# Attention denominators: summing four steps instead of two before the matmul with ones

## The chip, the cores and the metric

The kernel runs on one core of one Trainium2 chip. The metric is the device time of one execution in microseconds (us). Three runs of the kernel before gave 4889.07, 4887.17 and 4884.74 us, so the median is 4887.17 us.

A core has five engines that follow their own instruction lists and meet only at semaphores: TensorE (PE, matrix multiply, writes PSUM), VectorE (DVE), ScalarE (ACT), GpSimd (POOL) and the SyncE queue (SP) that issues transfers. PEld is the loading of weights into TensorE.

## The reference, cut to what matters

The whole kernel is a chain of four layers on x of shape 16 x 128 x 32 x 32. The change lies in one block, the attention of the third layer, on 16 batches of 1024 tokens:

```python
sq = (x @ wq_s).reshape(b, n, S, DH).transpose(0, 2, 1, 3) * scale     # S = 8 heads, DH = 16
sk = (x @ wk_s).reshape(b, n, S, DH).transpose(0, 2, 1, 3)
rv = (x @ wv_r).reshape(b, n, R, DH).transpose(0, 2, 1, 3)             # R = 2 retrievals
search_sim = jnp.einsum('bsid,bsjd->bsij', sq, sk)
search_attn = jax.nn.softmax(search_sim, axis=-1)
retrieved = jnp.einsum('bsij,brjd->bsird', search_attn, rv)
...
out = jnp.einsum('bsir,bsird->bsid', retrieval_attn, retrieved)
return out.transpose(0, 2, 1, 3).reshape(b, n, S * DH) @ w_out
```

The softmax over j (1024 keys) needs a sum of exponentials for each query i: the denominator. It is this sum that the change computes in another order.

## The kernel before, in words

`phase_attn` works through 16 batches. A batch has 32 steps `k`. A step takes one block of 128 keys for four heads and 512 queries, and eight steps in a row cover all 1024 keys of those heads and queries, so four groups of eight steps make a batch. All loops over batches are unrolled by two.

In step `k` TensorE does, in this order (function `slot` of the tensor block):

- four times a score matmul of step `k + 2` (`score`, into one of three PSUM tiles `at_S`), and between them the side work of step `k`. Scores run two steps ahead.
- the side work (`fill`): in almost every step four tiles of scores of the next batch, from which the row maxima are taken ("max"), and in a few steps transposes that finish an earlier half batch ("tokens", "back"), the output matmul ("wout") and the row offsets ("rows"). Side tiles go round three PSUM banks `at_side`.
- in every second step, in the middle of the step, `totals`: four matmuls with a matrix of ones that add 128 keys of a pair sum into `at_den`.
- `values`: four matmuls of the exponentials with the values, into `at_num`.

ScalarE (`exps`) turns the scores of a step into exponentials, tile by tile, into one of four slots `at_P`. A score matmul waits until the exponential three tiles back has been taken. At an even step `exps` also waits (`pair_done`) until the pair that used those slots four steps earlier has been added.

GpSimd (`pair`) adds the slots of two steps, 128 x 2048 elements, into `at_pairs` 0 or 1: pair `i` belongs to steps `2i` and `2i + 1`. Between pairs it does one part of seven of the small retrieval attention (`retrieve`). VectorE (`drain`) takes the maximum of each "max" tile and empties the other side tiles in the order in which TensorE made them. So VectorE is always at the step of TensorE or just behind it, while ScalarE and GpSimd work on later steps.

Names and lines of the profile: `at_S` L1633 score, `at_side` L1600 "max" tile, `at_den` L1655 totals, `at_num` L1644 values, `at_P` L1772 exponential, `at_pairs` L1532 pair sum, `at_mx` L1699 maximum, L1545 to L1570 the parts of `retrieve`.

Of the kernel before, what the change touches and what calls it, by code (L numbers as in the profile page):

```python
# [13 lines left out]
ALU = mybir.AluOpType  # L14
# [4 lines left out]
B = 16  # L19
# [1292 lines left out]
SIDES = 3  # L1312
RING = 3
HEADS = STEPS * 4
TOKENS_AT = (3, 19)
BACK_AT = (5, 22)
WOUT_AT = (6, 23)
EXP_AT = (28, 12)
SUM_AT = (30, 14)
MAX_AT = 19  # L1320
ROWS_AT = (27, 3, 11, 19)
GROUP = 32
# [44 lines left out]
def phase_attn(nc, K, D, X):  # L1367
# [6 lines left out]
    with Mem(nc, "at") as m:  # L1374
# [29 lines left out]
        side_ready, side_saved = m.sem("side_ready"), m.sem("side_saved")  # L1404
        s_ready, p_ready, pv_done = m.sem("s_ready"), m.sem("p_ready"), m.sem("pv_done")
        pair_done, den_done = m.sem("pair_done"), m.sem("den_done")
        num_saved, den_saved = m.sem("num_saved"), m.sem("den_saved")
        row_step, row_ready = m.sem("row_step"), m.sem("row_ready")
        far_ready = m.sem("far_ready")
# [46 lines left out]
        with nc.Block() as block:  # L1456
# [65 lines left out]
            @block.gpsimd  # L1522
            def _(g):
                for u in range(2):
                    g.memset(ko[u][KQ:KM, :, :], 1.0).then_inc(const_ready, 1)

                def pair(b, i):

                    wait_if(g, den_done, 16 * b + i - 1)
                    g.wait_ge(p_ready, HEADS * b + 8 * i + 8)  # L1530
                    a = 2 * i % SLOTS
                    g.tensor_tensor(pairs[i % 2][:, :, :], P[a][:, :, :], P[a + 1][:, :, :], ALU.add).then_inc(pair_done, 1)  # L1532

                def retrieve(b, h, part, tokens):

                    done = (0, 1, 4, 7, 7, 9, 10)[part]
                    step = Chain(g, post_step, 11 * (2 * b + h) + done)
                    heads = prod[:, :, :].rearrange("p i (s d) -> p (i s) d", d=DH)
                    nv = numT[:, :, :].rearrange("p i (s r d) -> p (i s) r d", r=RH, d=DH)
                    pv = prod[:, :, :].rearrange("p i (s r d) -> p (i s) r d", r=RH, d=DH)  # L1540
                    rec = recT
                    if part == 0:
                        g.wait_ge(side_saved, tokens)
                        g.wait_ge(u_in[h], 16 * b + 16)
                        step(g.tensor_tensor(pv, nv, ub[h][:, :, :].rearrange("p i (s o d) -> p (i s) o d", o=1, d=DH)  # L1545
                                             .to_broadcast([C, 32, RH, DH]), ALU.mult))
                    elif part == 1:
                        for w in (8, 4, 2):
                            step(g.tensor_tensor(heads[:, :, 0:w], heads[:, :, 0:w], heads[:, :, w:2 * w], ALU.add))
                    elif part == 2:  # L1550
                        step(g.tensor_tensor(sim[:, :, :].rearrange("p s r -> p (s r)"), heads[:, :, 0], heads[:, :, 1], ALU.add))
                        step(g.tensor_tensor(sim[:, :, :], sim[:, :, :],
                                             rec[:, :].rearrange("p (s o) -> p s o", o=1).to_broadcast([C, 32, 2]), ALU.mult))

                        step(g.tensor_tensor(sm1[:, :], sim[:, :, 0], sim[:, :, 1], ALU.subtract))
                        g.sem_inc(sim_ready, 1)
                    elif part == 3:
                        g.wait_ge(e_ready, 2 * b + h + 1)
                        g.tensor_tensor(sm1[:, :], sim[:, :, 0], sim[:, :, 1], ALU.add).then_inc(esum_ready, 1)
                    elif part == 4:  # L1560
                        g.wait_ge(rsum_ready, 2 * b + h + 1)
                        step(g.tensor_tensor(sm1[:, :], sm1[:, :], rec[:, :], ALU.mult))
                        step(g.tensor_tensor(sim[:, :, :], sim[:, :, :],
                                             sm1[:, :].rearrange("p (s o) -> p s o", o=1).to_broadcast([C, 32, 2]), ALU.mult))
                    elif part == 5:
                        step(g.tensor_tensor(heads, numT[:, :, :].rearrange("p i (s d) -> p (i s) d", d=DH),
                                             sim[:, :, :].rearrange("p s (r o) -> p (s r) o", o=1).to_broadcast([C, 64, DH]),
                                             ALU.mult))
                    else:
                        step(g.tensor_tensor(ub[h][:, :, :].rearrange("p i (s d) -> p (i s) d", d=DH),  # L1570
                                             pv[:, :, 0, :], pv[:, :, 1, :], ALU.add))
                        g.sem_inc(out_ready, 1)

                def slot(b, u, last):
                    post = not is_first(b)
                    for i in range(16):
                        pair(b, i)
                        if i == 0 and post:
                            retrieve(b - 1, 0, 6, None)
                        if 2 <= i <= 8 and post:  # L1580
                            retrieve(b - 1, 1, i - 2, side_at(b, ("tokens", 1, 3), last))
                        if i >= 10:
                            retrieve(b, 0, i - 10, side_at(b, ("tokens", 0, 3), last))

                over(g, B, slot)
                retrieve(B - 1, 0, 6, None)
                for part in range(7):
                    retrieve(B - 1, 1, part, TAIL_BASE + 4)

            @block.tensor  # L1590
            def _(pe):
# [55 lines left out]

                def totals(b, k):

                    j = (k - 2) % 8  # L1650
                    if j == 0:
                        wait_if(pe, den_saved, 4 * b + k // 8)
                    pe.wait_ge(pair_done, 16 * b + k // 2)
                    for i in range(QUAD):
                        last = pe.matmul(den[32 * i:32 * i + 32, :], K["ones"][:, 0:32], pairs[(k // 2 - 1) % 2][:, i, :],  # L1655
                                         start=(j == 0), stop=(j == 6))
                    last.then_inc(den_done, 1)

                for n in range(LEAD):
# [6 lines left out]
                def slot(b, u, last):  # L1666
# [5 lines left out]
                    for k in range(STEPS):  # L1672
                        if not last and k in (MAX_AT, MAX_AT + 8):
                            pe.wait_ge(op_in[1 - u][(k - MAX_AT) // 8], loads(b + 1, 1 - u))
                        work = side_work(k, first, last)
                        ahead_of = (b, u, k + 2) if k + 2 < STEPS else None if last else (b + 1, 1 - u, k + 2 - STEPS)
                        for i in range(QUAD):
                            if ahead_of:
                                score(*ahead_of, i)
                            for w in work[(i * len(work) + 2) // 4:((i + 1) * len(work) + 2) // 4]:  # L1680
                                fill(w, b, u, side_free(b, at), at % SIDES).then_inc(side_ready, 1)
                                at += 1
                            if i == 1 and k % 2 == 0 and not (first and k == 0):
                                totals(b, k)
                        values(b, u, k)

                over(pe, B, slot)
                totals(B, 0)
                for at, w in enumerate(TAIL):
                    fill(w, B, 0, side_free(B, at), at % SIDES).then_inc(side_ready, 1)  # L1690

# [1 line left out]
            def _(v):  # L1693
                def drain(w, b, u, at, bank):
# [36 lines left out]
                    else:  # L1731
                        xb = X[:, bass.ds((b - 1) * N + w[1] * CH, CH)]
                        v.tensor_tensor(xb, xb, side[bank][:, :], ALU.add).then_inc(side_saved, 1)

                def invert(job):
                    v.wait_ge(esum_ready, job + 1)
                    v.reciprocal(sm1[:, :], sm1[:, :]).then_inc(rsum_ready, 1)
# [5 lines left out]
                def slot(b, u, last):  # L1743
                    first = is_first(b)
                    at = 0
                    for k in range(STEPS):
                        if k == SUM_AT[1] and not first:
                            invert(2 * b - 1)
                        if k == SUM_AT[0]:
                            invert(2 * b)  # L1750
                        for w in side_work(k, first, last):
                            drain(w, b, u, side_base(b) + at, at % SIDES)
                            at += 1

                over(v, B, slot)
                for at, w in enumerate(TAIL):
                    if w == ("back", 1):
                        invert(2 * B - 1)
                    drain(w, B, 0, TAIL_BASE + at, at % SIDES)

            @block.scalar
            def _(a):
# [11 lines left out]
                def save(b, g, what):  # L1774
# [6 lines left out]
                            a.wait_ge(side_ready, side_at(b, ("tokens", 1 - half, 3), isinstance(b, int) and b == B - 1))  # L1781
                        a.copy(sums[:, quad, :], num[:, :]).then_inc(num_saved, 1)
                    else:
                        a.wait_ge(den_done, 16 * b + 4 * g + 4)
                        a.copy(sums[:, 2 + quad, :], den[:, :]).then_inc(den_saved, 1)

                def softmax2(job):
# [7 lines left out]
                def slot(b, u, last):  # L1795
# [2 lines left out]
                        exps(b, 0)  # L1798
                    for k in range(STEPS):
                        saved = None  # L1800
                        if k % 8 < 2 and (k >= 8 or not first):
                            saved = (b, k // 8 - 1, k % 8) if k >= 8 else (b - 1, 3, k % 8)
                        if k + 1 < STEPS:
                            exps(b, k + 1, saved)
                        elif not last:
# [1012 lines left out]
```

## Time and profile before

| | |
|---|---|
| median of three runs | 4887.17 us |
| the profiled execution | 4881.74 us |
| its span, first to last instruction | 4879.9 us |
| busy PE, DVE, ACT, POOL over the span | 86%, 60%, 45%, 37% |
| mean granted TensorE clock | 0.921 |

The page gives busy shares over the whole program, which runs through several phases; what the attention block does is read from its own stretch. The attention steps lie between 1258 and 3216 us of the span. A granted clock of 1.0 is 2.4 GHz, one of 0.5 is 1.2 GHz. Busy time of PE counts a pipelined matmul up to its end, so two matmuls in a row overlap, and the distance between their starts is what one costs.

### The profile page before, as it was taken

To read this page: it belongs to the slowest core of one execution; us is meant where nothing else is said; L and a number is where in the kernel's file an instruction comes from. 1 tells how busy PE (TensorE), PEld (TensorE's weight loads), DVE (VectorE), ACT (ScalarE), POOL (GpSimd) and SP (SyncE) were. 2 spreads that over 40 slices of the span, in tenths; PEclk is the share of its full clock that TensorE was granted. 3 is DMA by queue.
4 is the path that set the end of the run, shared out by engine and by line. 5 is a ranking of instruction groups with operands and counts; after the bars stand their busy time and mean duration, and the time that the engine had idled before them with its cause. 6 is when DMAs were issued, how large, how long until landed. Compare 5 with 4: busy or idle time off the path is not lost. (4 is left out here: it accounts for less than half of the span.)

```text
span 4879.9 us, 76343 instructions
## 1 busy us (share of the span) xinstructions
PE 4184.0 (86%) x23099; PEld 1656.3 (34%) x23099; DVE 2925.3 (60%) x5621; ACT 2181.0 (45%) x4040; POOL 1827.4 (37%) x1333
## 2 busy tenths in 40 slices
PE   5799999846999999999999999967999999876513
PEld 2343433324222222222222222234444444453312
DVE  4788888656777777777777777742000000256774
ACT  3333333245466656565656566653333333431400
POOL 1100000037477777777777777771000000220401
PEclk9999999979899999999999999988999999966655
DMA  3555645357322222222222222010000000111504
GB/s 138 138 137 118 140 115 136 74 195 253 42 33 33 33 33 33 33 33 33 33 33 33 33 33 33 6 61 29 0 0 0 0 0 0 74 65 47 190 0 151
DMA packets 201952, 313.47 MB, mean 64 GB/s; under 512 B 48887, under 2 KB 132861, under 8 KB 199181
## 3 DMA queue, kind: packets, MB, share of 16 engines
q1 hardware_dynamic: 172296, 270.23, 23.8%
q10 hardware_dynamic: 24960, 28.87, 1.7%
q0 software_dynamic: 4368, 10.07, 0.7%
q8 instruction: 197, 3.23, 0.3%
q14 instruction: 131, 1.07, 0.1%
HBM read 102.88 MB, written 78.12 MB: 37 GB/s over the span
## 5 line engine op out<-in xcount | busy, mean ns | idle before, releaser
L1699 DVE TENSOR_REDUCE at_mx<-at_side 128x1 f32<-128x512 f32 x2048 | 1295.6, 682 | 410.0 <-PE at_side L1600 402.5
L1772 ACT ACTIVATE at_P<-at_S 128x512 f32<-128x512 f32 x2048 | 1115.2, 600 | 702.3 <-PE at_S L1633 692.6
L1532 POOL TENSOR_TENSOR at_pairs<-at_P 128x2048 f32<-128x2048 f32 x256 | 1159.9, 4531 | 238.5 <-ACT at_P L1772 210.7
L1633 PE MATMUL at_S<-at_qo,at_ko 99*128 99x512 bf16 x2048 | 788.2, 387 | 73.3 <-ACT at_P L1772 47.6
L1600 PE MATMUL at_side<-at_ko,at_qo 96*128 96x512 bf16 x2048 | 775.8, 389 | 29.3 <-DMA at_ko<-qk 24.1
L2054 ACT ACTIVATE ff_hs<-ff_ph,ff_b 128x512 f32<-128x512 f32 x512 | 351.7, 687 | 524.4 <-PE ff_ph L2024 524.4
L1644 PE MATMUL at_num<-at_P,at_rvt 128*32 128x512 f32 x4096 | 557.5, 606 | 0.0
L2024 PE MATMUL ff_ph<-ffn_Y,ff_w 128*128 (+1 forms) x1024 | 524.8, 594 | 8.7 <-DMA ff_b<-in_b_dram 8.7
L2038 PE MATMUL ff_po<-ff_hs,ff_w2s 128*128 128x512 f32 x1024 | 522.5, 592 | 0.0
L2073 DVE SCALAR_TENSOR_TENSOR X<-ff_po,ffn_b2w,X 128x512 f32 (+1 forms) x32 | 24.0, 751 | 822.9 <-PE ff_po L2038 822.9
L834 DVE SCALAR_TENSOR_TENSOR la_dwq<-la_pad,la_taps,la_dwq 128x1024 f32<-128x1024 f32 x384 | 491.4, 1280 | 11.1
L1633 PEld LDWEIGHTS at_S<-at_qo,at_ko 99*128 99x128 bf16 x2048 | 198.2, 97 | 879.3 <-ACT at_P L1772 658.0
L1108 POOL TENSOR_TENSOR n_ln_ab<-n_ln_mv,eps 128x4 f32<-128x4 f32 x96 | 19.1, 199 | 1161.0 <-DVE n_ln_mv L1099 1158.3
L582 POOL DMA_DIRECT2D proj<-la_y x32 | 17.4, 544 | 810.3 <-ACT la_y L941 810.3
L619 PE MATMUL la_acc<-la_rep,la_wagg 128*32 128x512 f32 x2560 | 314.6, 609 | 3.8 <-DMA la_rep<-la_pad 3.1
L1600 PEld LDWEIGHTS at_side<-at_ko,at_qo 96*128 96x128 bf16 x2048 | 200.9, 98 | 272.0 <-DVE at_mx L1699 95.0
L2024 PEld LDWEIGHTS ff_ph<-ffn_Y,ff_w 128*128 128x128 f32 x1024 | 195.3, 191 | 254.4 <-issue 245.0
L1655 PE MATMUL at_den<-at_pairs,ones 128*32 128x512 f32 x2048 | 277.3, 614 | 4.5 <-POOL at_pairs L1532 4.4
L2038 PEld LDWEIGHTS ff_po<-ff_hs,ff_w2s 128*128 128x128 f32 x1024 | 194.6, 190 | 245.2 <-issue 244.7
L1123 ACT ACTIVATE n_ln_xt<-n_ln_front,n_ln_ab 128x128 f32<-128x128 f32 x384 | 144.4, 456 | 114.2 <-POOL n_ln_ab L1114 103.8
L1644 PEld LDWEIGHTS at_num<-at_P,at_rvt 128*32 128x32 f32 x4096 | 91.3, 108 | 174.7 <-issue 104.3
L1545 POOL TENSOR_TENSOR at_prod<-at_numT,at_ub 128x1024 f32<-128x1024 f32 x32 | 75.5, 2358 | 185.0 <-DVE at_recT L1728 185.0
(416 smaller groups left out, 4596.4 us busy)
## 6 DMA issues: line engine op xcount, KB each, us to landing
la_rep<-la_pad SPq DMA_DIRECT2D x512, 162.8 KB, 3.6
qk<-ap_part SPq DMA_DIRECT2D x32, 768.0 KB, 3.7
at_qo<-qk SPq DMA_DIRECT2D x384, 64.0 KB, 3.7
at_ko<-qk SPq DMA_DIRECT2D x192, 128.0 KB, 5.8
n_ln_xs<-X SPq DMA_DIRECT2D x96, 256.0 KB, 2.3
u<-ap_us SPq DMA_DIRECT2D x32, 320.0 KB, 4.0
X<-in_x_dram SPq DMA_DIRECT2D x4, 2048.0 KB, 25.6
conv<-conv_Y SPq DMA_DIRECT2D x16, 512.0 KB, 2.6
```

Source lines behind the costliest of these rows:

```text
L619: done = pe.matmul(acc[c][32 * j:32 * j + 32, :], wagg[:, p - 1, j, g, :], view(slice(0, C), p, h, j, *PLACES[g]), start=(c < 2 and g == 0 ...
L834: v.scalar_tensor_tensor(out, image, taps[:, t:t + 1], out, ALU.mult, ALU.add).then_inc(tap_done, 1)
L1532: g.tensor_tensor(pairs[i % 2][:, :, :], P[a][:, :, :], P[a + 1][:, :, :], ALU.add).then_inc(pair_done, 1)
L1600: return pe.matmul(side[bank][:, :], qo[of_u][0:KQ, i // QUAD, s, i % QUAD * C:(i % QUAD + 1) * C], ko[of_u][0:KQ, s, h * CH:(h + 1) * CH] ...
L1633: pe.matmul(S[n % RING][:, :], ko[u][:, h, j * C:(j + 1) * C], qo[u][:, half, h, :], start=True, stop=True).then_inc(s_ready, 1)
L1644: last = pe.matmul(num[32 * i:32 * i + 32, :], rvt[u][:, j, :], P[k % SLOTS][:, i, :], start=(j == 0), stop=(j == 7))
L1655: last = pe.matmul(den[32 * i:32 * i + 32, :], K["ones"][:, 0:32], pairs[(k // 2 - 1) % 2][:, i, :], start=(j == 0), stop=(j == 6))
L1699: v.reduce_max(mx[:, n // 2, n % 2:n % 2 + 1], side[bank][:, :], AX.X).then_inc(side_saved, 1)
L1772: a.activation(P[k % SLOTS][:, i, :], S[(4 * k + i) % RING][:, :], ACT.Exp).then_inc(p_ready, 1)
L2024: pe.matmul(ph[j % R][:, :], w1[:, f, :], Y[:, bass.ds(b * N + half * CH, CH)], start=True, stop=True).then_inc(h_mm, 1)
L2038: done = pe.matmul(po[half][:, :], w2s[u][:, f, :], hs[j % R][:, :], start=(f == 0), stop=(f == FT - 1)).then_inc(h_used, 1)
L2054: a.activation(hs[j % R][:, :], ph[j % R][:, :], ACT.Gelu, bias=b1[:, j % FT:j % FT + 1]).then_inc(h_ready, 1)
```

## The change

The pair sums are added once more before the matmul with ones: the sum of an even pair (`at_pairs0`) is added onto the sum of the odd pair after it (`at_pairs1`), so that `totals` runs once for four steps. The second addition has 128 x 2048 elements too. GpSimd does its left half (two of four heads, 128 x 1024) right behind the odd pair; VectorE does the right half as two instructions of 128 x 512 (`right`), one at the end of steps 4, 8, 12, ..., one behind the second side tile of steps 5, 9, 13, ... The next even pair waits for both halves, the next odd pair for `totals`. Positions of other work are moved by the table of constants and in the lists of GpSimd and ScalarE.

```diff
-TOKENS_AT = (3, 19)
-BACK_AT = (5, 22)
-WOUT_AT = (6, 23)
-EXP_AT = (28, 12)
-SUM_AT = (30, 14)
+TOKENS_AT = (4, 20)
+BACK_AT = (9, 25)
+WOUT_AT = (10, 26)
+EXP_AT = (30, 14)
+SUM_AT = (31, 16)
...
                 def pair(b, i):
 
-                    wait_if(g, den_done, 16 * b + i - 1)
+                    if i % 2 == 0:
+                        wait_if(g, quad_right, 16 * b + i)
+                        wait_if(g, quad_left, 8 * b + i // 2)
+                    else:
+                        wait_if(g, den_done, 8 * b + i // 2)
                     g.wait_ge(p_ready, HEADS * b + 8 * i + 8)
                     a = 2 * i % SLOTS
                     g.tensor_tensor(pairs[i % 2][:, :, :], P[a][:, :, :], P[a + 1][:, :, :], ALU.add).then_inc(pair_done, 1)
+                    if i % 2:
+                        g.wait_ge(pair_done, 16 * b + i + 1)
+                        g.tensor_tensor(pairs[1][:, 0:2, :], pairs[1][:, 0:2, :], pairs[0][:, 0:2, :], ALU.add).then_inc(quad_left, 1)
...
-                        if i == 0 and post:
-                            retrieve(b - 1, 0, 6, None)
-                        if 2 <= i <= 8 and post:
-                            retrieve(b - 1, 1, i - 2, side_at(b, ("tokens", 1, 3), last))
-                        if i >= 10:
-                            retrieve(b, 0, i - 10, side_at(b, ("tokens", 0, 3), last))
+                        if i < 2 and post:
+                            retrieve(b - 1, 0, 5 + i, None)
+                        if 3 <= i <= 9 and post:
+                            retrieve(b - 1, 1, i - 3, side_at(b, ("tokens", 1, 3), last))
+                        if i >= 11:
+                            retrieve(b, 0, i - 11, side_at(b, ("tokens", 0, 3), last))
...
                 def totals(b, k):
 
-                    j = (k - 2) % 8
-                    if j == 0:
-                        wait_if(pe, den_saved, 4 * b + k // 8)
-                    pe.wait_ge(pair_done, 16 * b + k // 2)
+                    q = (k - 6) // 4
+                    if q % 2 == 0:
+                        wait_if(pe, den_saved, 4 * b + q // 2)
+                    pe.wait_ge(quad_left, 8 * b + q + 1)
+                    pe.wait_ge(quad_right, 16 * b + 2 * q + 2)
...
-                            if i == 1 and k % 2 == 0 and not (first and k == 0):
+                            if i == 1 and k % 4 == 2 and not (first and k == 2):
                                 totals(b, k)
...
+                def right(b, q, i):
+
+                    v.wait_ge(pair_done, 16 * b + 2 * q + 2)
+                    v.tensor_tensor(pairs[1][:, i, :], pairs[1][:, i, :], pairs[0][:, i, :], ALU.add).then_inc(quad_right, 1)
...
-                        for w in side_work(k, first, last):
+                        work = side_work(k, first, last)
+                        for i, w in enumerate(work):
                             drain(w, b, u, side_base(b) + at, at % SIDES)
                             at += 1
+                            if i == min(1, len(work) - 1) and k % 4 == 1 and not (first and k == 1):
+                                right(b, (k - 5) // 4, 3)
+                        if not work and k % 4 == 1:
+                            right(b, (k - 5) // 4, 3)
+                        if k % 4 == 0 and not (first and k == 0):
+                            right(b, (k - 4) // 4, 2)
...
-                        if k % 8 < 2 and (k >= 8 or not first):
-                            saved = (b, k // 8 - 1, k % 8) if k >= 8 else (b - 1, 3, k % 8)
+                        if k % 8 in (0, 3) and (k >= 8 or not first):
+                            what = int(k % 8 == 3)
+                            saved = (b, k // 8 - 1, what) if k >= 8 else (b - 1, 3, what)
```

On GpSimd, at the start of a batch, the list of the kernel before goes through the pairs (L1532) with a part of the retrieval between them:

```order
L1532 TENSOR_TENSOR at_pairs1<-at_P2,at_P3 128x2048
L1566 TENSOR_TENSOR at_prod<-at_numT,at_sim 128x1024
L1532 TENSOR_TENSOR at_pairs0<-at_P0,at_P1 128x2048
L1570 TENSOR_TENSOR at_ub1<-at_prod 128x512
...
L1545 TENSOR_TENSOR at_prod<-at_numT,at_ub0 128x1024
```

The same place of GpSimd's list in the changed kernel, from one even pair to the next (L1537 is the pair, L1540 the left half of the second addition):

```order
L1537 TENSOR_TENSOR at_pairs0<-at_P0,at_P1 128x2048
L1537 TENSOR_TENSOR at_pairs1<-at_P2,at_P3 128x2048
L1540 TENSOR_TENSOR at_pairs1<-at_pairs1,at_pairs0 128x1024
L1553 TENSOR_TENSOR at_prod<-at_numT,at_ub0 128x1024
...
L1557 TENSOR_TENSOR at_prod<-at_prod 128x64x8
```

An instruction of 128 x 1024 now stands behind every odd pair, and the even pair that follows writes the tile `at_pairs0` that VectorE's halves read.

On VectorE, in steps 8 and 9 of a batch, the changed kernel has the two instructions of `right` (L1748) between the maxima (L1709) of the side tiles; before, the eight maxima followed each other. Each row names the bank of the side tile that it empties:

```order
L1709 TENSOR_REDUCE at_mx<-at_side2 128x1
L1709 TENSOR_REDUCE at_mx<-at_side0 128x1
L1709 TENSOR_REDUCE at_mx<-at_side1 128x1
L1748 TENSOR_TENSOR at_pairs1<-at_pairs1,at_pairs0 128x512
L1709 TENSOR_REDUCE at_mx<-at_side2 128x1
L1709 TENSOR_REDUCE at_mx<-at_side0 128x1
L1748 TENSOR_TENSOR at_pairs1<-at_pairs1,at_pairs0 128x512
L1709 TENSOR_REDUCE at_mx<-at_side1 128x1
```

The first `right` stands behind the last maximum of step 8, the second behind the second maximum of step 9.

## Rows read from the trace of the kernel before

**Rows 1.** The page's groups: out<-in count | busy, mean ns | idle before, releaser

```profile
L1699 DVE TENSOR_REDUCE at_mx<-at_side 128x1 f32<-128x512 f32 x2048 | 1295.6, 682 | 410.0 <-PE at_side L1600 402.5
L1772 ACT ACTIVATE at_P<-at_S 128x512 f32<-128x512 f32 x2048 | 1115.2, 600 | 702.3 <-PE at_S L1633 692.6
L1532 POOL TENSOR_TENSOR at_pairs<-at_P 128x2048 f32<-128x2048 f32 x256 | 1159.9, 4531 | 238.5 <-ACT at_P L1772 210.7
L1655 PE MATMUL at_den<-at_pairs,ones 128*32 128x512 f32 x2048 | 277.3, 614 | 4.5 <-POOL at_pairs L1532 4.4
```

**Rows 2.** Tile at_S: ns min/median/max of an instruction, first and last start

```profile
L1633 PE MATMUL at_S<-at_qo,at_ko x2048: 377/381/634, 1258.3 to 3214.9; 99*128 99x512 bf16 x187
```

**Rows 3.** Waits, 1258 to 3230 us: who for whom, us in total, times, longest

```profile
PE at_S L1633 <- ACT at_P L1772: 47.6, 66, 1.4
...
ACT at_P L1772 <- POOL at_pairs L1532: 1.5, 2, 1.1
```

**Rows 4.** Windows, one batch: us; busy PE, PEld, DVE, ACT, POOL; clock, DMA

```profile
1625.00:1748.00 123.00, 114.40 (x676) 33.56 (x668) 90.44 (x167) 72.29 (x138) 91.41 (x41) 0.99 0.23 34
```

**Rows 5.** Timeline of two plain steps: start, duration, engine, instruction, idle before

```profile
1753.79 0.39 PE L1633 MATMUL at_S<-at_qo,at_ko 99*128 99x512 bf16 x1
...
1754.44 2.48 DVE L1699 TENSOR_REDUCE at_mx<-at_side 128x1 f32<-128x512 f32 x4 [0.69 <-PE at_side L1600]
...
1755.11 0.38 PE L1633 MATMUL at_S<-at_qo,at_ko 99*128 99x512 bf16 x1
...
1756.64 0.39 PE L1633 MATMUL at_S<-at_qo,at_ko 99*128 99x512 bf16 x1
...
1757.61 1.06 PE L1655 MATMUL at_den<-at_pairs,ones 128*32 128x512 f32 x8
...
1758.61 0.39 PE L1633 MATMUL at_S<-at_qo,at_ko 99*128 99x512 bf16 x1
```

**Rows 6.** Timeline around the latest pair of a batch, steps 21 to 24

```profile
1701.67 2.40 ACT L1772 ACTIVATE at_P<-at_S 128x512 f32<-128x512 f32 x4 [0.89 <-PE at_S L1633]
...
1709.37 4.53 POOL L1532 TENSOR_TENSOR at_pairs<-at_P 128x2048 f32<-128x2048 f32 x1 [0.23 <-POOL at_prod L1545]
...
1713.49 0.39 PE L1633 MATMUL at_S<-at_qo,at_ko 99*128 99x512 bf16 x1
...
1714.18 2.07 ACT L1772 ACTIVATE at_P<-at_S 128x512 f32<-128x512 f32 x4
...
1714.84 0.39 PE L1633 MATMUL at_S<-at_qo,at_ko 99*128 99x512 bf16 x1 [0.74 <-ACT at_P L1772]
```

**Rows 7.** Groups of GpSimd by shape: the costliest part of retrieve

```profile
L1545 POOL TENSOR_TENSOR at_prod<-at_numT,at_ub 128x1024 f32<-128x1024 f32 x32 | 75.5, 2358 | 185.0 <-DVE at_recT L1728 185.0
```

**Rows 8.** Groups of VectorE by shape: additions with both inputs in SBUF

```profile
L2539 DVE TENSOR_TENSOR sk_tmp<-sk_G,sk_vv 128x1024 f32<-128x1024 f32 x8 | 9.8, 1225 | 0.3
...
L761 DVE TENSOR_TENSOR X<-X,la_res 128x512 f32<-128x512 f32 x8 | 5.1, 684 | 0.0
```

**Rows 9.** Timeline of PE: matmuls that start after an idle time

```profile
750.50 5.82 PE L598 MATMUL la_acc<-X,la_wqkv 128*128 x9 [2.05 <-issue]
...
1748.13 0.60 PE L1633 MATMUL at_S<-at_qo,at_ko 99*128 99x512 bf16 x1 [4.47 <-issue]
```

**Rows 10.** Windows, columns as in Rows 4, behind and around those idle times

```profile
751.71:755.12 3.41, 3.41 (x5) 1.35 (x4) 3.30 (x4) 1.35 (x3) 0.00 (x0) 0.51 0.97 208
1745.00:1750.00 5.00, 1.86 (x8) 0.56 (x12) 0.69 (x1) 1.27 (x3) 4.62 (x2) 0.50 1.11 134
```

**Rows 11.** Timeline: a VectorE copy within SBUF beside a GpSimd memset

```profile
4587.63 1.80 POOL L2413 MEMSET sk_zeros<- 128x2048 f32 x1 [0.15 <-POOL sk_gw L2411]
4587.80 1.71 DVE L2509 COPY sk_same_e<-sk_emask 128x128 f32<-128x128 f32 x1
```

**Rows 12.** Timeline: VectorE products with both inputs in SBUF beside GpSimd

```profile
138.09 6.43 POOL L571 TENSOR_SCALAR_AFFINE_SELECT la_plain<-la_plain 32x128 f32<-32x128 f32 x8
...
140.28 3.02 DVE L784 TENSOR_TENSOR la_wagg<-la_pwt,la_dwt 128x1280 f32<-128x1280 f32 x2
```

More of the change, by code:

```diff
@@ L1406, in phase_attn @@
         pair_done, den_done = m.sem("pair_done"), m.sem("den_done")
+        quad_left, quad_right = m.sem("quad_left"), m.sem("quad_right")
         num_saved, den_saved = m.sem("num_saved"), m.sem("den_saved")
@@ L1577, in slot @@
                         pair(b, i)
-                        if i == 0 and post:
-                            retrieve(b - 1, 0, 6, None)
-                        if 2 <= i <= 8 and post:
-                            retrieve(b - 1, 1, i - 2, side_at(b, ("tokens", 1, 3), last))
-                        if i >= 10:
-                            retrieve(b, 0, i - 10, side_at(b, ("tokens", 0, 3), last))
+                        if i < 2 and post:
[4 more added lines that the diff above has]
+                            retrieve(b, 0, i - 11, side_at(b, ("tokens", 0, 3), last))
                 over(g, B, slot)
-                retrieve(B - 1, 0, 6, None)
+                for part in range(5, 7):
+                    retrieve(B - 1, 0, part, None)
                 for part in range(7):
@@ L1648, in totals @@
                 def totals(b, k):
-                    j = (k - 2) % 8
-                    if j == 0:
-                        wait_if(pe, den_saved, 4 * b + k // 8)
-                    pe.wait_ge(pair_done, 16 * b + k // 2)
+                    q = (k - 6) // 4
[3 more added lines that the diff above has]
+                    pe.wait_ge(quad_right, 16 * b + 2 * q + 2)
                     for i in range(QUAD):
-                        last = pe.matmul(den[32 * i:32 * i + 32, :], K["ones"][:, 0:32], pairs[(k // 2 - 1) % 2][:, i, :],
-                                         start=(j == 0), stop=(j == 6))
+                        last = pe.matmul(den[32 * i:32 * i + 32, :], K["ones"][:, 0:32], pairs[1][:, i, :],
+                                         start=(q % 2 == 0), stop=(q % 2 == 1))
                     last.then_inc(den_done, 1)
@@ L1687, in _ @@
                 over(pe, B, slot)
-                totals(B, 0)
+                totals(B, 2)
                 for at, w in enumerate(TAIL):
@@ L1750, in slot @@
                             invert(2 * b)
-                        for w in side_work(k, first, last):
+                        work = side_work(k, first, last)
+                        for i, w in enumerate(work):
                             drain(w, b, u, side_base(b) + at, at % SIDES)
                             at += 1
+                            if i == min(1, len(work) - 1) and k % 4 == 1 and not (first and k == 1):
[4 more added lines that the diff above has]
+                            right(b, (k - 4) // 4, 2)
                 over(v, B, slot)
+                for i in range(2, 4):
+                    right(B, -1, i)
                 for at, w in enumerate(TAIL):
@@ L1783, in save @@
                     else:
-                        a.wait_ge(den_done, 16 * b + 4 * g + 4)
+                        a.wait_ge(den_done, 8 * b + 2 * g + 2)
                         a.copy(sums[:, 2 + quad, :], den[:, :]).then_inc(den_saved, 1)
```

## The prediction

> **What bounds the kernel now.** First the page's groups, for the size of each instruction of the attention block [rows 1], then the tile `at_S`, for how long the block lasts. Its first score starts at 1258.3 us and its last at 3214.9 [rows 2]: 1956.6 us for 16 batches of 32 steps, which is 15.29 us for four steps (a quad; there are 128). All terms below are per quad.
>
> The windows of one batch show no idle engine to spare except ScalarE: of 123 us PE is busy 114, DVE 90, POOL 91 and ACT 72 [rows 4]. The timeline of plain steps gives TensorE's price. A step without totals runs from 1753.79 to 1756.64, 2.85 us; a totals group occupies it from 1757.61 to 1758.61, 1.00 us [rows 5]. A quad with two totals is 4 x 2.85 + 2 x 1.00 = 13.4 us. The other 1.9 us of the 15.29 are the tokens, back, wout and rows work, the restart of the loop every second batch and short waits. So TensorE's own list bounds the block. The waits agree: the scores wait 47.6 us in all for exponentials, and ScalarE waits 1.5 us in all for a pair [rows 3].
>
> That GpSimd holds nobody up rests on slack, and the slack can be read. Pair 11 (steps 22 and 23) is the latest of its batch. The exponentials of step 23 end at 1701.67 + 2.40 = 1704.07, in TensorE's step 21, but the pair starts only at 1709.37, since GpSimd had waited for tokens, and ends at 1713.90. Step 24 of TensorE begins at 1713.49, and the exponentials that reuse the slots begin at 1714.18 [rows 6]. So a pair may start as late as the end of the step behind the one in which its last operand was scored (here step 22), and no later: these 5.3 us were just early enough.
>
> **The change part by part.**
>
> *TensorE loses work.* The 2048 rows of L1655 [rows 1] are 256 totals groups of 8; half go, one per quad: 1.00 us less. Its list falls from 13.4 to 12.4 us.
>
> *GpSimd gains the left half*, 128 x 1024. With 2.36 us for 1024 columns [rows 7] and 4.53 for 2048 [rows 1], I take 2.3 us (an estimate; L1545 reads in a more broken pattern, so it is at the upper end). Its load per batch goes from 91.4 to 91.4 + 8 x 2.3 = 110 us, 13.7 per quad: more than TensorE's plain list, less than 15.29. By load alone it fits.
>
> *VectorE gains two additions of 128 x 512* at 0.68 us each [rows 8]. Load per batch: 90.4 + 16 x 0.68 = 101 us, 12.7 per quad. Fits too.
>
> *The new wait is what counts.* The even pair of a quad (steps 0 and 1 of the quad) now waits until VectorE has added both halves of the quad before. The second of these stands behind the second side tile of step 1, and VectorE gets a side tile only when TensorE has computed it in step 1. But the exponentials of step 1 are done two steps earlier, while TensorE is in step 3 of the quad before. So an even pair can no longer start early. It starts when TensorE is at the end of step 1, and its 4.53 us then lie across step 2, in which TensorE scores the next quad's step 0, whose exponentials need the slots of this very pair. By rows 6 the latest harmless start was the end of step 0. Queued behind the waiting pair are the retrieval part, the odd pair and the next left half; ScalarE waits for the pair, TensorE for ScalarE.
>
> This closes a loop whose length is the period of a quad:
> - even pair 4.53 [rows 1];
> - first exponential of the next step 0: 0.60 [rows 1];
> - from the fourth score of step 2, which waits for that exponential (three score tiles go ahead), to the end of step 2: 1756.64 - 1755.11 = 1.53 [rows 5];
> - step 3: 2.85;
> - from the start of the next step 0 to its first maximum: 1754.44 - 1753.79 = 0.65 [rows 5];
> - four maxima 2.48 [rows 5], first addition 0.68, two maxima of step 1 1.24 (half of 2.48), second addition 0.68.
>
> The sum is 15.24. Three changes of engine (VectorE to GpSimd, to ScalarE, to TensorE) at about 0.1 each make 15.5; one is read as 1714.84 - 1714.18 - 0.60 = 0.06 [rows 6]. TensorE's list of 12.4 us lies beside it, so TensorE stands still for 3.1 us in every step 2. The totals that were saved fall into that hole and buy nothing.
>
> *Extras.* Of the 1.9 us beyond the plain list, some falls on the loop (tokens in steps 0 and 3, the rows work on VectorE in step 3 which delays step 0's maxima, the copy of `at_num` in step 0, long retrieval parts before the odd pair) and some into the hole (tokens and wout in step 2). Bounds 0 and 1.9; I take half, 0.95, since two of the four steps lie on the loop whole and two in part.
>
> *The clock.* TensorE now idles 3.1 us at a stretch. Before two matmuls of the trace it had idled 2.05 and 4.47 us [rows 9], and the granted clock was 0.51 in the 3.41 us behind the first and 0.50 around the second [rows 10]: 1.2 in place of 2.4 GHz. Such a stretch costs half of 3.41 us, 1.7, where TensorE works through it, and nothing where it stands still anyway. Bounds 0 and 1.7; I take 0.9, in the middle, because the slow stretch begins partly inside the hole, and steps 2 and 3 behind it lie on the loop.
>
> *Moved positions.* Tokens one step later, back and wout three or four, each part of the retrieval one pair later, the two copies into `at_sums` apart: as many instructions as before. They cost nothing while GpSimd waits for VectorE anyway; were that cover gone, the longest part, 2.36 us [rows 7], would delay an odd pair, which is counted among the extras. At the end one left half and two additions follow the last pair, some 4 us once.
>
> Sum: 15.5 + 0.95 + 0.9 = 17.35 against 15.29, 2.06 more; times 128 is 264 us. The profiled execution took 4881.7 us (span 4879.9), so 5146; the median of the runs is 5.4 above it. With that, 5150.
>
> **The rivals.**
>
> 1. *Only the loop.* Extras all in the hole, no clock loss: 15.5, 0.2 us x 128 = 27 us more, about 4915; with a part of the extras up to 5000. For it: the clock stood at 0.99 over a batch that is full of short waits [rows 4]. Against it: the rows work lies in step 3 of every second quad, and 2.05 us of idling were enough to lose the clock [rows 9, 10].
>
> 2. *VectorE's additions are held by GpSimd.* A copy within SBUF of 128 x 128 took 1.71 us and ended at 4589.51, with a GpSimd memset that ended at 4589.43 [rows 11]; it seems to have waited it out. Against: two products with two SBUF inputs, 128 x 1280, took 3.02 us, 1.51 each, beside GpSimd selects without a gap [rows 12], just what 684 and 1225 ns for 512 and 1024 columns [rows 8] extrapolate to (1.50). If held, the first addition waits for the left half or a retrieval part under way, from 0 to 2.3 us; the second does not, as GpSimd then waits for it. Since GpSimd's work behind the odd pair ends near the time of the first addition, I take 0.6: 77 us more than forecast, 5225; at the upper end 5440.
> The Trainium skill, "SBUF — State Buffer", section "SBUF: two separate sides", says that a VectorE instruction with two SBUF inputs and a GpSimd instruction that reads SBUF exclude each other for a whole instruction. By that rule it is this rival. Rows 11 agree with an exclusion, rows 12 do not.
>
> 3. *Faster.* If the new wait ended before the pair could start anyway, TensorE's list would still bind: 15.29 - 1.00 = 14.3, 128 us less, 4754. For it: every engine's load fits into 14.3 (GpSimd 13.7). It decides by whether the second addition ends before the end of step 0; its place in VectorE's list, behind two side tiles of step 1, speaks against.
>
> **How the numbers follow.** Forecast (loop, extras, some clock; 5000 to 5310) 0.68; rival 1 0.11; rival 2 0.10; rival 3 0.11. Range 4940 to 5310: the lower end leaves out rival 3 and the bottom of rival 1, the upper end takes in the middle of rival 2. The largest sum of the upper bounds, 15.5 + 1.9 + 1.7 + 2.3 = 21.4, would be 5670 and is left out. About 10 us (0.2%) is what runs of this kernel can tell from no change. Faster: rival 3, 0.11. Same: the very bottom of rival 1, 0.03. Slower 0.86.
>
> **What would show it.** In the profile after: GpSimd's pair waits for VectorE's `at_pairs` some 100 times, hundreds of us in all; ScalarE's wait for `at_pairs` grows from 1.5 us to several hundred (about 4 us x 128); the scores' wait for `at_P` on TensorE grows by about 3 us x 128; the clock in a batch falls from 0.99 to about 0.9 or less; L1655 has 1024 rows. Extras and clock can be told apart by the length of step 3. An addition of VectorE that lasts much over 0.7 us speaks for rival 2. ScalarE without a wait for `at_pairs` would prove me wrong.

## The result, and the profile after

The changed kernel took 5242.77 us (median of four runs, 5232.06 to 5251.3), the kernel before on the same chip 4885.95 us (four runs, 4883.24 to 4889.07). The ratio is 1.0729 [1.0704, 1.0754]: slower by 357 us, where 264 were forecast. The profiled execution has a span of 5234.2 us and a mean granted clock of 0.888, against 4879.9 and 0.921.

The tile `at_S` of the changed kernel gives the length of the block (ns min/median/max, first and last start):

```profile
L1642 PE MATMUL at_S<-at_qo,at_ko x2048: 379/389/634, 1258.0 to 3560.0; 99*128 99x512 bf16 x187
```

That is 2302.0 us in place of 1956.6 [rows 2], 17.98 us per quad in place of 15.29: 345 of the 354 us by which the span grew lie here.

The page's groups that answer to [rows 1] (out<-in count | busy, mean ns | idle before, releaser), with the two halves of the second addition:

```profile
L1709 DVE TENSOR_REDUCE at_mx<-at_side 128x1 f32<-128x512 f32 x2048 | 1308.2, 682 | 608.6 <-PE at_side L1609 604.6
L1796 ACT ACTIVATE at_P<-at_S 128x512 f32<-128x512 f32 x2048 | 1107.9, 605 | 1057.9 <-POOL at_pairs L1537 661.5
L1537 POOL TENSOR_TENSOR at_pairs<-at_P 128x2048 f32<-128x2048 f32 x256 | 1155.3, 4518 | 570.5 <-ACT at_P L1796 323.7
...
L1540 POOL TENSOR_TENSOR at_pairs<-at_pairs 128x1024 f32<-128x1024 f32 x128 | 302.3, 2362 | 10.0
...
L1748 DVE TENSOR_TENSOR at_pairs<-at_pairs 128x512 f32<-128x512 f32 x256 | 190.4, 744 | 13.6 <-POOL at_pairs L1537 13.6
```

No engine fills the new length: over the block PE is busy 1941 of 2302 us, GpSimd 1743, VectorE 1605 (first window below). What grew is idle time; the three old groups shown here all have more of it, and their instructions are about as long as before. The additions of VectorE, 744 ns in the mean, are longer than the 684 ns of [rows 8].

The waits of the changed kernel over the block (who for whom, us in total, times, longest), against [rows 3]:

```profile
ACT at_P L1796 <- POOL at_pairs L1537: 661.5, 158, 5.0
...
PE at_S L1642 <- ACT at_P L1796: 330.4, 218, 3.0
POOL at_pairs L1537 <- ACT at_P L1796: 323.7, 86, 46.2
...
POOL at_pairs L1537 <- DVE at_pairs L1748: 240.6, 58, 15.3
```

ScalarE waited 1.5 us for pairs before and waits 661.5 now. The pair's own wait is split over two names. A wait for several semaphores is put down to the one that came last by the profile, which here is often ScalarE's exponential; but that exponential belongs to a later step than the pair. In the 124 quads where the timeline shows all of it, the even pair starts 0.22 us (mean) behind the end of VectorE's second addition.

One turn of the loop in the timeline (start, duration, engine, instruction, idle before), from step 0 into the next step 3:

```profile
1694.02 0.68 DVE L1748 TENSOR_TENSOR at_pairs<-at_pairs 128x512 f32<-128x512 f32 x1
...
1694.73 1.29 DVE L1709 TENSOR_REDUCE at_mx<-at_side 128x1 f32<-128x512 f32 x2
...
1695.94 0.68 DVE L1748 TENSOR_TENSOR at_pairs<-at_pairs 128x512 f32<-128x512 f32 x1
...
1696.87 4.51 POOL L1537 TENSOR_TENSOR at_pairs<-at_P 128x2048 f32<-128x2048 f32 x1 [4.02 <-DVE at_pairs L1748]
...
1701.49 1.08 ACT L1796 ACTIVATE at_P<-at_S 128x512 f32<-128x512 f32 x2 [4.91 <-POOL at_pairs L1537]
...
1702.15 0.61 PE L1642 MATMUL at_S<-at_qo,at_ko 99*128 99x512 bf16 x1 [2.63 <-ACT at_P L1796]
...
1703.11 1.94 PE L1653 MATMUL at_num<-at_P,at_rvt 128*32 128x512 f32 x8
...
1720.39 0.39 PE L1642 MATMUL at_S<-at_qo,at_ko 99*128 99x512 bf16 x1 [1.73 <-ACT at_P L1796]
...
1720.93 1.06 PE L1653 MATMUL at_num<-at_P,at_rvt 128*32 128x512 f32 x8
```

Addition, two maxima, addition, pair, exponential, score: each row starts within 0.3 us of the end of the one before it (for the score, of the first of the two exponentials), and GpSimd, ScalarE and TensorE had stood idle 4.02, 4.91 and 2.63 us until then. Behind the idle time of 2.63 us the eight value matmuls took 1.94 us, one quad later, behind 1.73 us, 1.06. The granted clock was 0.50 around the first, which is 1.2 GHz, and 1.00 around the second.

Windows of the changed kernel: the whole block, those two places, and two stretches of 135 us (columns as in [rows 4]):

```profile
1258.00:3560.00 2302.00, 1941.28 (x9925) 550.12 (x9925) 1605.47 (x2903) 1173.68 (x2262) 1742.78 (x746) 0.91 0.17 25
1703.00:1705.00 2.00, 2.00 (x10) 0.23 (x10) 0.88 (x2) 1.05 (x3) 1.84 (x2) 0.50 1.14 125
1720.90:1722.10 1.20, 1.20 (x10) 0.31 (x10) 0.69 (x1) 0.91 (x2) 1.20 (x1) 1.00 0.00 0
...
1651.00:1786.00 135.00, 113.73 (x626) 33.56 (x626) 100.43 (x186) 73.36 (x142) 108.87 (x49) 0.97 0.21 30
2056.00:2191.00 135.00, 113.54 (x563) 33.57 (x560) 91.02 (x166) 65.11 (x125) 100.34 (x43) 0.87 0.20 30
```

The clock is not lost evenly: 0.97 in one stretch, 0.87 in another, 0.91 over the block, where it was 0.99 before.

### The profile page after: what moved, and what is told of

Same layout as the page of the kernel before. It is cut to its first block and busy times, and to the rows that moved or that the text cites. A ratio compares the mean times of both kernels' runs of the same rounds, so it can differ in the third digit from the quotient of the medians.

```text
span 5234.2 us, 74930 instructions
## 1 busy us (share of the span) xinstructions
PE 4247.1 (81%) x22075; PEld 1662.8 (32%) x22075; DVE 3090.6 (59%) x5877; ACT 2166.2 (41%) x4040; POOL 2136.8 (41%) x1461
## 5 line engine op out<-in xcount | busy, mean ns | idle before, releaser
L1709 DVE TENSOR_REDUCE at_mx<-at_side 128x1 f32<-128x512 f32 x2048 | 1308.2, 682 | 608.6 <-PE at_side L1609 604.6
L1796 ACT ACTIVATE at_P<-at_S 128x512 f32<-128x512 f32 x2048 | 1107.9, 605 | 1057.9 <-POOL at_pairs L1537 661.5
L1537 POOL TENSOR_TENSOR at_pairs<-at_P 128x2048 f32<-128x2048 f32 x256 | 1155.3, 4518 | 570.5 <-ACT at_P L1796 323.7
L1642 PE MATMUL at_S<-at_qo,at_ko 99*128 99x512 bf16 x2048 | 848.1, 416 | 362.3 <-ACT at_P L1796 330.4
L1609 PE MATMUL at_side<-at_ko,at_qo 96*128 96x512 bf16 x2048 | 811.6, 416 | 28.7 <-DMA at_ko<-qk 24.3
L1653 PE MATMUL at_num<-at_P,at_rvt 128*32 128x512 f32 x4096 | 625.8, 674 | 0.0
L834 DVE SCALAR_TENSOR_TENSOR la_dwq<-la_pad,la_taps,la_dwq 128x1024 f32<-128x1024 f32 x384 | 491.3, 1279 | 11.1
L1540 POOL TENSOR_TENSOR at_pairs<-at_pairs 128x1024 f32<-128x1024 f32 x128 | 302.3, 2362 | 10.0
L1748 DVE TENSOR_TENSOR at_pairs<-at_pairs 128x512 f32<-128x512 f32 x256 | 190.4, 744 | 13.6 <-POOL at_pairs L1537 13.6
```

The source lines that it names most:

```text
L834: v.scalar_tensor_tensor(out, image, taps[:, t:t + 1], out, ALU.mult, ALU.add).then_inc(tap_done, 1)
L1540: g.tensor_tensor(pairs[1][:, 0:2, :], pairs[1][:, 0:2, :], pairs[0][:, 0:2, :], ALU.add).then_inc(quad_left, 1)
L1609: return pe.matmul(side[bank][:, :], qo[of_u][0:KQ, i // QUAD, s, i % QUAD * C:(i % QUAD + 1) * C], ko[of_u][0:KQ, s, h * CH:(h + 1) * CH] ...
L1642: pe.matmul(S[n % RING][:, :], ko[u][:, h, j * C:(j + 1) * C], qo[u][:, half, h, :], start=True, stop=True).then_inc(s_ready, 1)
L1653: last = pe.matmul(num[32 * i:32 * i + 32, :], rvt[u][:, j, :], P[k % SLOTS][:, i, :], start=(j == 0), stop=(j == 7))
L1709: v.reduce_max(mx[:, n // 2, n % 2:n % 2 + 1], side[bank][:, :], AX.X).then_inc(side_saved, 1)
```

## The experiments

The theory was the loop: even pair, exponential, rest of step 2, step 3, the maxima and additions up to the second addition, and round again, with a clock loss in the hole of step 2. The main rival was that VectorE's additions and GpSimd's instructions hold each other up; another was that the moved positions cost something. All times below are medians; ratios are to the kernel before on the same chip (4886.71 us, seven runs, for the first four; 4887.97, seven runs, for the last two).

**Both additions one position earlier.** They stand at the end of step 0, so the loop loses the two maxima of step 1:

```diff
-                            if i == min(1, len(work) - 1) and k % 4 == 1 and not (first and k == 1):
-                                right(b, (k - 5) // 4, 3)
...
                         if k % 4 == 0 and not (first and k == 0):
-                            right(b, (k - 4) // 4, 2)
+                            for i in range(2, 4):
+                                right(b, (k - 4) // 4, i)
```

> Both additions of VectorE stand at the end of step 0 of a quad; the second no longer waits behind two maxima of step 1. Loop theory: the two maxima (1.24 us) leave the loop and TensorE's hole in step 2 gets as much shorter, with some clock back: 1.2 to 1.8 us per quad, 128 quads, so 5010 to 5090 us. Rival (the added load on GpSimd and VectorE and their exclusion is the cost, not the place of the wait): within 15 us of 5243.

One run: 4980.48 us, clock 0.918; 262 us less than the changed kernel, and below the loop's expectation. Its waits over the block:

```profile
ACT at_P L1793 <- POOL at_pairs L1537: 487.9, 158, 4.9
...
POOL at_pairs L1537 <- DVE at_pairs L1748: 181.1, 81, 11.4
...
PE at_S L1642 <- ACT at_P L1793: 145.6, 159, 3.3
```

The loop is still closed, only shorter. The block's scores start from 1257.0 to 3303.4 us: 15.99 per quad, 1.99 less. The two maxima are 1.24 of it. Over the block the clock is 0.98 in place of 0.91, so most of the other 0.75 is likely the clock; that is argued, not measured apart. Against the kernel with the hole filled (below), whose clock is as high, the move is worth 17.03 - 15.99 = 1.04 us.

**Additions before the even pair needs them.** Both at the end of step 3 of their own quad, which should open the loop altogether:

```diff
...
+                        if k % 4 == 3:
+                            for i in range(2, 4):
+                                right(b, (k - 3) // 4, i)
...
```

> Both additions of VectorE stand at the end of step 3 of their own quad, a whole step and a half earlier. Loop theory: the even pair can start about when its operands are ready, the loop no longer sets the period, and TensorE's list with half the totals (14.3 us) or GpSimd and VectorE taking turns (about 15.1 us if they exclude each other) does: 4760 to 4870 us, ScalarE's wait for pairs under 100 us, clock near 0.98. Rival (added load and exclusion cost the time): above 5000 us.

5305.5 us, ratio 1.0854 [1.0818, 1.089]: slower than the changed kernel, and the loop's expectation failed. The waits of this kernel:

```profile
POOL at_pairs L1537 <- PE at_den L1665: 415.7, 117, 6.6
...
PE at_side L1609 <- DVE at_mx L1709: 208.2, 89, 3.1
...
ACT at_P L1791 <- POOL at_pairs L1537: 11.1, 4, 4.8
```

The additions of this kernel (tile `at_pairs`, ns min/median/max):

```profile
L1748 DVE TENSOR_TENSOR at_pairs<-at_pairs x256: 676/1379/2851, 1273.2 to 3648.1; 128x512 f32<-128x512 f32 x128
```

And its timeline at one pair of additions:

```profile
2029.21 2.35 POOL L1540 TENSOR_TENSOR at_pairs<-at_pairs 128x1024 f32<-128x1024 f32 x1
...
2030.02 2.09 DVE L1748 TENSOR_TENSOR at_pairs<-at_pairs 128x512 f32<-128x512 f32 x1
...
2031.52 2.79 POOL L1553 TENSOR_TENSOR at_prod<-at_numT,at_ub 128x1024 f32<-128x1024 f32 x1
...
2032.03 2.83 DVE L1748 TENSOR_TENSOR at_pairs<-at_pairs 128x512 f32<-128x512 f32 x1
...
2035.52 0.61 PE L1609 MATMUL at_side<-at_ko,at_qo 96*128 96x512 bf16 x1 [3.11 <-DVE at_mx L1709]
```

Two additions of 0.68 us take 4.84. The first ends 0.55 us behind the left half's end (2031.56); then the retrieval part, 2.36 us elsewhere, takes 2.79, and the second ends 0.55 behind that (2034.86). The maxima behind them in VectorE's list come late, TensorE finds no free side bank for 3.11 us, and the totals, which stand in step 2 of a TensorE that is now late, hold the odd pair: 117 of the 128 odd pairs wait for them. These additions in turn wait for the odd pair, so this is a loop again, over the other wait that the change brought in. ScalarE's wait for pairs is down to 11.1 us, as the loop theory wanted; the bound that takes its place is dearer. Part of the time is the clock, 0.86 over the block against 0.91 in the changed kernel; how much was not taken apart.

**The hole filled.** The changed kernel with two more groups of totals per quad, on weights of zero, in step 2 (2.0 us of TensorE work more per quad, the sums unchanged):

```diff
...
+                    for _ in range(2):
+                        last = group(nothing[:, :], False, False)
...
```

> The changed kernel with two more groups of totals matmuls on zero weights behind the real one, in step 2 of each quad: 2.0 us more work for TensorE per quad, 256 us in all, put where it stands still. Loop theory with a clock cost: the hole absorbs the work, the granted clock stays up (0.90 to about 0.97 in the block) and the time falls by 0.5 to 1.5 us per quad, to 5050 to 5180 us. Loop theory without a clock cost: 5243, within 15 us. Rival (TensorE's work still sets the period): 256 us more, 5500 us.

5115.77 us, ratio 1.0467 [1.045, 1.0485], clock 0.922: 127 us less than the changed kernel although it does 256 us of matmuls more. The waits for the loop stay (GpSimd's pair is L1540 in this kernel, the exponential L1807):

```profile
ACT at_P L1807 <- POOL at_pairs L1540: 669.9, 163, 5.0
```

The window of the whole block, in this kernel:

```profile
1260.00:3440.00 2180.00, 2000.85 (x11941) 590.50 (x11941) 1598.13 (x2903) 1163.20 (x2261) 1749.03 (x746) 0.99 0.18 27
```

The clock is 0.99, as in the kernel before (1.00 and 0.95 in the two stretches of 135 us). The loop alone thus costs 17.03 us per quad (scores from 1260.4 to 3440.2 us), and the clock that the changed kernel loses 0.95 on top.

**Positions only.** The kernel before with the changed table of constants and the moved parts of the retrieval, without the second addition:

```diff
-TOKENS_AT = (3, 19)
+TOKENS_AT = (4, 20)
...
-                        if 2 <= i <= 8 and post:
+                        if 3 <= i <= 9 and post:
```

> The kernel before with only the moved positions of the change (tokens, back, wout, exponentials and reciprocals of the retrieval, and its parts one pair later); sums of two steps and all totals as before. Forecast: positions cost nothing, 4886 us within 15. Rival: they are part of the loss, above 4920 us.

One run: 4880.12 us, clock 0.921; the runs of before lie between 4880.9 and 4890.76. These moves cost nothing in the kernel before. The moved copies of ScalarE into `at_sums` are not among them, and in the changed kernel no run takes the moves apart.

**Additions in the middle of step 0,** both behind its second side tile:

```diff
-                            if i == min(1, len(work) - 1) and k % 4 == 1 and not (first and k == 1):
-                                right(b, (k - 5) // 4, 3)
+                            if i == min(1, len(work) - 1) and k % 4 == 0 and not (first and k == 0):
+                                for half in range(2, 4):
+                                    right(b, (k - 4) // 4, half)
...
```

> Both additions of VectorE behind the second side tile of step 0. Loop theory alone: two more maxima (1.24 us) leave the loop compared with the end of step 0 (period 15.99 us there), which brings it to about 14.7, near TensorE's own list: 4790 to 4850 us. If VectorE's addition and a GpSimd instruction that reads SBUF exclude each other: the additions now come while the left half (2.36 us) runs on GpSimd, last over 1 us on average in place of 0.74, VectorE falls behind and TensorE waits for side tiles: 4880 to 5050 us.

5014.3 us, ratio 1.0259 [1.0242, 1.0276], clock 0.909. By the loop alone it should have beaten the end of step 0, and it is 34 us slower than that one run; it lies where exclusion was to bring it. Its waits, and its additions:

```profile
ACT at_P L1796 <- POOL at_pairs L1537: 213.6, 106, 4.9
...
POOL at_pairs L1537 <- DVE at_pairs L1748: 116.8, 78, 8.3
POOL at_pairs L1537 <- PE at_den L1665: 108.5, 54, 5.1
```

```profile
L1748 DVE TENSOR_TENSOR at_pairs<-at_pairs x256: 677/781/2864, 1279.1 to 3345.6; 128x512 f32<-128x512 f32 x128
```

ScalarE's wait for pairs falls to a third of the changed kernel's, and odd pairs wait for totals. The additions last 1.12 us in the mean, as expected under exclusion. The loop is still there: 107 of 127 even pairs start within 0.4 us behind the second addition. The clock over the block is 0.96, against 0.98 with the additions at the end of step 0, so that part of the 34 us is the clock too.

**All of the second addition on VectorE,** two instructions of 128 x 1024 in the same place, nothing of it on GpSimd:

```diff
-                        g.tensor_tensor(pairs[1][:, 0:2, :], pairs[1][:, 0:2, :], pairs[0][:, 0:2, :], ALU.add).then_inc(quad_left, 1)
...
-                    v.tensor_tensor(pairs[1][:, i, :], pairs[1][:, i, :], pairs[0][:, i, :], ALU.add).then_inc(quad_right, 1)
+                    v.tensor_tensor(pairs[1][:, 2 * i:2 * i + 2, :], pairs[1][:, 2 * i:2 * i + 2, :], pairs[0][:, 2 * i:2 * i + 2, :], ALU.add).then_inc(quad_right, 1)
...
```

> The whole second addition on VectorE, as two instructions of 128 x 1024 behind the second side tile of step 0; GpSimd does only pairs and the retrieval. The loop is then 4.53 + 0.60 + 1.53 + 2.85 + 0.65 + 1.24 + 2.45 (two of 1.225) + 0.3 = 14.2 us and there is no left half to be excluded by. Loop with exclusion: 4780 to 4890 us, the additions near 1.23 us each, faster than the variant with the left half on GpSimd at the same place. Rival (VectorE's load, 11.3 + 2.45 = 13.8 us per quad in bursts, holds up the side tiles): 4900 to 5050 us.

4997.09 us, ratio 1.0223 [1.0206, 1.024]; the expectation of 4780 to 4890 failed. Its waits, and its additions:

```profile
POOL at_pairs L1536 <- DVE at_pairs L1743: 287.6, 69, 11.9
...
ACT at_P L1791 <- POOL at_pairs L1536: 223.8, 128, 3.5
...
PE at_side L1605 <- DVE at_mx L1704: 101.5, 150, 1.3
POOL at_pairs L1536 <- PE at_den L1660: 98.6, 49, 2.2
```

```profile
L1743 DVE TENSOR_TENSOR at_pairs<-at_pairs x256: 1210/1217/3353, 1280.5 to 3338.4; 128x1024 f32<-128x1024 f32 x128
```

With no left half beside them the additions keep their size in the median (1217 ns; 1225 in [rows 8]). But 2.4 us in one place of VectorE's list delay the maxima behind, and TensorE waits for side banks 150 times. That is 101.5 us, 0.8 per quad, and does not fill the gap between the 14.2 us expected and the 16.16 measured (scores from 1260.0 to 3328.3 us). The loop is closed here too: all 127 even pairs start within 0.4 us behind the second addition. The additions take the 2.5 us of the sum; the stretch from the even pair to the values of step 2 takes 6.9 us, where the changed kernel has 5.95, and the one from the values of step 3 to the first addition 3.7, where the sum has 2.9. What makes them longer was not followed further.

No version with the second addition beat the kernel before. A third tile for pair sums, so that the even pair need not wait for VectorE, was not tried.

## Why the prediction was right, and where it was off

*The loop* was right: in 126 of 127 quads of the changed kernel the even pair starts within 0.4 us behind the second addition. The timeline gives its parts, as means over the 124 quads that it shows whole (even pair to the first value matmul of step 2; from there to step 3's values; to the first addition; to the next even pair), and beside them the same parts of the forecast and of the kernel with the hole filled:

| us per quad | forecast's 15.5 | hole filled | changed kernel |
|---|---|---|---|
| even pair to values of step 2 | 5.87 | 5.88 | 5.95 |
| to values of step 3 | 2.85 | 3.14 | 3.94 |
| to the first addition | 4.12 | 5.12 | 5.25 |
| to the next even pair | 2.70 | 3.00 | 2.96 |
| sum | 15.5 | 17.1 | 18.1 |

The forecast's column is its own sum cut at these points: 4.53 + 0.60 + two hand-overs + 0.54 (1720.93 - 1720.39); then step 3; then 1.0 of values and 0.65 + 2.48 of step 0; then 0.68 + 1.24 + 0.68 + 0.1. The sums differ by 0.1 from the block's 17.03 and 17.98, which take in its edges.

*The extras* are the term that was mis-sized. I took 0.95, half of the 1.9 us that lay beyond TensorE's plain list, "since two of the four steps lie on the loop whole and two in part". With the hole filled 1.5 is left (17.03 - 15.5), two thirds of it between the values of step 3 and the first addition, most of which is step 0. One of its causes in the timeline of the changed kernel:

```profile
1725.51 0.59 ACT L1806 COPY at_sums<-at_num 128x512 f32<-128x512 f32 x1 [1.90 <-PE at_num L1653]
...
1726.65 0.39 PE L1642 MATMUL at_S<-at_qo,at_ko 99*128 99x512 bf16 x1 [0.74 <-ACT at_P L1796]
...
1727.29 1.89 DVE L1709 TENSOR_REDUCE at_mx<-at_side 128x1 f32<-128x512 f32 x3 [0.66 <-PE at_side L1609]
...
1729.09 0.68 DVE L1748 TENSOR_TENSOR at_pairs<-at_pairs 128x512 f32<-128x512 f32 x1
```

ScalarE's copy of `at_num`, which I listed among the extras, waits for the values of step 3; the exponentials behind it come late, TensorE's second score waits 0.74, the second side tile and with it the maxima 0.66, and so the first addition. Step 0 lies on the loop with everything that delays its maxima. The copy is not the main part: it stands in every second quad, and with the hole filled the stretch to the first addition takes 5.2 us in these and 5.0 in the others. The longest, 6.9 us, is that of the last quad of a batch, which runs into the next batch. What else makes up the 1.0 us was not taken apart.

*The clock* was right in place and size: 0.9 forecast, 0.95 measured by filling the hole, 0.80 of it in step 3 by the table. That the middle of the bounds 0 and 1.7 came so near is in part luck, since the clock is lost so unevenly. Together 15.5 + 1.53 + 0.95 = 17.98. The 0.58 too little per quad in the extras (17.03 - 15.5 - 0.95) is 74 of the 93 us that the forecast missed. The rest is small: 128 times 0.05 for the clock, and some 9 us of span outside the block, of which the forecast named 4 and added none.

*The saved totals bought nothing*, as forecast: 1024 instead of 2048 of them, and TensorE only waits longer. The hole came out near its size: `at_S` waits for exponentials 283 us more than before, 2.2 us per quad. The 3.1 forecast were the loop's 15.5 less a list of 12.4 that held none of the side work beyond the plain steps.

*Rival 1*, only the loop, fell by the clock and the extras. *Rival 3*, faster, fell with 661.5 us of waits for pairs.

*Rival 2*, VectorE's additions held by GpSimd, was rightly left out of the time and wrongly argued. Its 5225 us lie nearer to the 5243 measured than the forecast's 5150, so the time alone does not decide against it; the length of the additions does. The exclusion exists. In the changed kernel's timeline:

```profile
1812.28 2.36 POOL L1540 TENSOR_TENSOR at_pairs<-at_pairs 128x1024 f32<-128x1024 f32 x1
...
1814.22 0.97 DVE L1748 TENSOR_TENSOR at_pairs<-at_pairs 128x512 f32<-128x512 f32 x1
...
1814.60 0.75 POOL L1559 TENSOR_TENSOR at_sim<-at_prod 128x64 f32<-128x64 f32 x1
```

The addition, 0.68 us elsewhere, waits for the left half's end at 1814.64 and takes 0.97; the small GpSimd product waits for the addition's end at 1815.19 and takes 0.75 in place of 0.29. The Trainium skill, "SBUF — State Buffer", section "SBUF: two separate sides", says that a VectorE instruction with two SBUF inputs and a GpSimd instruction that reads SBUF shut each other out for a whole instruction, and here the trace agrees.

The forecast took [rows 12] as evidence against it, and that was misread: it looked at the products alone. The same place of the kernel before, with the selects one by one:

```profile
139.06 0.39 POOL L571 TENSOR_SCALAR_AFFINE_SELECT la_plain<-la_plain 32x128 f32<-32x128 f32 x1
...
140.28 1.49 DVE L784 TENSOR_TENSOR la_wagg<-la_pwt,la_dwt 128x1280 f32<-128x1280 f32 x1
140.56 1.46 POOL L571 TENSOR_SCALAR_AFFINE_SELECT la_plain<-la_plain 32x128 f32<-32x128 f32 x1
```

One select took 0.39 us; the one that starts 0.28 us behind the start of a product took 1.46 and ended 0.25 behind the product. The product had begun first and was not held; the select was. So these rows, too, speak for the exclusion.

But in the changed kernel it lengthens the additions by 16 us in all ((744 - 681) ns x 256) and the small GpSimd products by 14 ((731 - 291) ns x 31), since the additions come so late that GpSimd mostly stands waiting for them. Moved earlier, the additions run into GpSimd's work and pay.

## What to carry to other kernels

When a tile of a pipelined producer gets a second reader, follow that reader's place in its engine's list round to the producer: if the producer's own output feeds the work that the reader stands behind, the wait is a loop, and where it is longer than every engine's own list, its length is the period. Work saved on the engine that such a loop leaves idle buys nothing. Moving the reader earlier only helps until it meets what ran beside it, so price the instructions that it will then overlap. A row that shows one engine unhurt is half a reading: look at the other engine's instruction beside it.

## What had not been expected of the hardware

Adding 256 us of matmuls on zero weights made the kernel 127 us faster: the mean granted clock rose from 0.888 to 0.922, and in the block from 0.91 to 0.99, with TensorE at work in the hole where it had stood still, 2.63 us in the quad shown. A VectorE addition with both inputs in SBUF and a GpSimd instruction that reads SBUF took turns for whole instructions, in both directions: 0.68 us became up to 2.85, a GpSimd product of 2.36 took 2.79, and a GpSimd select of 0.39 took 1.46.
